# Self-attention of a decoder kernel: rounded three-product projections, values for two heads at a time, output projection with stationary weights

## The reference

```python
# one head of 16, per sequence of 56 tokens
q = n @ Wq[h] + bq[h]          # 448 x 128
k = n @ Wk[h] + bk[h]
v = n @ Wv[h] + bv[h]
s = q @ k.T + slope[h] * alibi # causal
p = softmax(s)
y += (p @ v) @ Wo[h]           # 448 x 256
# after all heads
x = x + y + bo
```

## Time and profile before

| | us |
|---|---|
| median of 3 runs | 560.01 |
| lowest and highest | 556.16, 560.06 |
| the profiled execution, its device time | 554.69 |
| its span, first to last instruction | 553.1 |
| TensorE busy in the span | 521.2 (94%) |
| VectorE busy | 338.2 (61%) |
| ScalarE busy | 297.1 (54%) |
| mean granted clock of TensorE | 0.985 |

### The profile page before, as it was taken

The page is one execution under the profiler, slowest core; times in us unless marked ns, Lnnn a source line. Parts: engine busy times, 40 slices in busy tenths (PEclk is TensorE's granted clock), DMA queues, the critical chain, the costliest instruction groups (busy, mean ns, idle before and its releaser), DMA issues.

```text
span 553.1 us, 16214 instructions
## 1 busy us (share of the span) xinstructions
PE 521.2 (94%) x7083; PEld 411.2 (74%) x7083; DVE 338.2 (61%) x757; ACT 297.1 (54%) x521; POOL 4.1 (1%) x12
## 2 busy tenths in 40 slices
PE   7999999999978999999999998999999899888897
PEld 6777777787857888878788877779778688645356
DVE  3335645665425676557665678855678764778961
ACT  3363655434325675557766667766557755353132
POOL 1000000000010000000000000000000000000000
PEclk9999999999979999999999999999999999899989
DMA  8821212212500211121111111111111100000000
GB/s 278 364 77 40 77 38 77 58 58 77 201 9 2 65 51 39 42 76 39 39 39 41 39 39 39 39 41 38 40 39 39 48 2 2 2 1 10 0 1 17
DMA packets 10791, 30.83 MB, mean 56 GB/s; under 512 B 1377, under 2 KB 4450, under 8 KB 9954
## 3 DMA queue, kind: packets, MB, share of 16 engines
q1 hardware_dynamic: 10274, 29.07, 16.1%
q0 software_dynamic: 192, 0.51, 0.3%
q10 hardware_dynamic: 256, 0.23, 0.1%
HBM read 29.35 MB, written 0.46 MB: 54 GB/s over the span
## 4 chain that ended last, share of the span: by engine, by line
PE 73%; DVE 11%; ACT 9%; issue 3%; DMA 2%; SPq 0%; DVEq 0%; ACTq 0%
PE psb L1213 10%; PE psb L1223 10%; PE psa L1145 8%; PE psa L1265 7%; PE psb L1283 5%; PE pst L1160 5%; PE psa L1153 5%; PE psb L1189 3%; PE psa L1169 2%; PE psb L1492 2%; ACT shared L520 2%; PE pst L1431 2%; DMA cst<-consts_dram 1%; PE psb L1180 1%; PE pst L1349 1%
## 5 line engine op out<-in xcount | busy, mean ns | idle before, releaser
L1213 PE MATMUL psb<-cx,wkv 128*128 128x500 f32 x288 | 78.1, 407 | 4.1 <-ACT vmem L371 4.1
L1223 PE MATMUL psb<-wkv,cx 128*125 128x256 f32 x552 | 77.5, 289 | 3.6 <-ACT kx L364 3.6
L1223 PEld LDWEIGHTS psb<-wkv,cx 128*125 128x125 f32 x552 | 68.4, 186 | 7.6 <-ACT kx L364 6.1
L1213 PEld LDWEIGHTS psb<-cx,wkv 128*128 128x128 f32 x288 | 50.6, 188 | 16.9 <-ACT vmem L371 4.6
L371 ACT ACTIVATE vmem<-psb 125x512 f32<-125x512 f32 x46 | 27.5, 597 | 57.9 <-PE psb L1223 57.9
L1265 PE MATMUL psa<-qb,kx 32*125 32x112 f32 x1536 | 54.7, 279 | 1.4 <-ACT vmem L371 0.8
L812 DVE TENSOR_SCALAR shared<-shared,top 125x896 f32<-125x896 f32 x48 | 30.8, 684 | 40.0 <-ACT shared L520 39.8
L313 ACT ACTIVATE shared<-shared,negmax 112x112 f32<-112x112 f32 x64 | 24.0, 376 | 55.0 <-DVE negmax L728 55.0
L1265 PEld LDWEIGHTS psa<-qb,kx 32*125 32x125 f32 x1536 | 46.3, 183 | 9.6 <-issue 4.8
L1145 PE MATMUL psa<-xnT,whd 128*128 128x448 f32 x128 | 50.9, 540 | 0.8 <-DVE xnT L662 0.8
L812 DVE TENSOR_SCALAR smem<-smem,top 125x896 f32<-125x896 f32 x48 | 30.8, 683 | 27.7 <-ACT smem L520 27.4
(11 more groups left out here) (299 smaller groups left out, 799.2 us busy)
## 6 DMA issues: line engine op xcount, KB each, us to landing
ring<-ctx_t_dram SPq DMA_DIRECT2D x24, 500.0 KB, 3.7
whd<-heads_dram SPq DMA_DIRECT2D x16, 385.0 KB, 3.2
whd<-heads_dram SPq DMA_DIRECT2D x16, 129.0 KB, 2.3
wraw<-w_dram SPq DMA_DIRECT2D x2, 1024.0 KB, 6.2
mats_sb<-mats_dram SPq DMA_DIRECT2D x1, 1536.0 KB, 14.6
wraw<-gate_dram SPq DMA_DIRECT2D x1, 1024.0 KB, 8.1
wraw<-up_dram SPq DMA_DIRECT2D x1, 1024.0 KB, 10.2
wraw<-down_dram SPq DMA_DIRECT2D x1, 1024.0 KB, 12.1
```

What stands on the lines that cost most here:

```text
L1213: last = nc.tensor.matmul(bank[:, 0:UT], wkv[a][:, 0, c, m * P:(m + 1) * P], cx[b][u % 2][:, c, :], start=(a == b and c == 0), stop=(a == ...
L1223: last = nc.tensor.matmul(bank[0:CT, t * D:(t + 1) * D], cx[b][u % 2][:, c, a0:a0 + CT], wkv[a][:, 1, c, :], start=(a == b and c == 0), st ...
```

## The change

- q and k are computed by three f32r products (`PARTS0`: HI x HI, LO x HI, HI x LO), 12 matmuls of 448 columns a head. The normalised x is divided once, into `x0[HI]` and `x0[LO]`. The weights of each head are divided during the loop: `split_qk(h + 2)` on ScalarE behind `pT` of head h, `rest_qk(h + 2)` on VectorE behind the normalisation of head h. The parts share memory with the context tiles `cx`.
- Values are computed for two heads at a time, 256 columns a matmul, in three products: `project_v(n, i)` is one tile of 112 tokens, 6 matmuls; head h issues `project_v(h + 2, 0)` before its transposes and `project_v(h + 2, 1)` behind them. The weights of a pair are divided by `split_v` and `rest_v` in odd heads.
- The output projection has the weights stationary: 2 matmuls of 448 columns, giving the transposed output `yT`. After the last head it is evicted with its bias by ScalarE and VectorE and turned back by `turn_y(t)`, once before the cross-attention and three times within its loop. The bias matmuls at the start are gone.
- Transfers: q and k weights, value weights of a pair, output weights and biases are separate; the load of `down` stands behind the loads of heads 2 and 3, each with a wait for the rests that free the buffers.
- Moved: `wkv[HI]` and `round_up(0)` from heads 7 and 8 to head 14, `round_up(1)` to head 15 between the exponentials and `pT`; `wkv[LO]` to head 14, `remainder(0)` to head 15, `remainder(1)` between `normalise1(0)` and `finish1(0)`.

```diff
+            load_qk(1)
+            load_v(1)
+            load_wo(0)
+            load_wo(1)
...
+            for i in range(2):
+                sp.wait_ge(s_wl, i + 1)
+                load_qk(2 + i)
+                sp.wait_ge(s_vl, i + 1)
+                load_v(2 + i)
             sp.dma_start(wraw[:, 2, :], down).then_inc(s_wff, 16)
...
+            def split_qk(h):
+                act.wait_ge(s_w[h % 2], 16 * (h // 2) + 16)
+                if h >= 2:
+                    act.wait_ge(s_q, 2 * h - 2)
+                nc.scalar.activation(cq[HI][h % 2], whd[h % 2][:, 0:QW], ACT.Copy).then_inc(s_wh, 1)
+
+            def split_v(j):
+                act.wait_ge(s_wv[j % 2], 16 * (j // 2) + 16)
+                if j >= 2:
+                    act.wait_ge(s_v, 2 * j - 2)
+                nc.scalar.activation(wkv[HI][:, j % 2, :, :], vraw[j % 2], ACT.Copy).then_inc(s_vh, 1)
...
             root(0, n=NT)
+            split_qk(0)
             act.wait_ge(s_nb, 1)
...
             for h in range(H0):
                 head(h)
+                if h + 2 < H0:
+                    split_qk(h + 2)
+                if h % 2 and (h + 3) // 2 < H0 // 2:
+                    split_v((h + 3) // 2)
...
+            def rest_qk(h):
+                dve.wait_ge(s_wh, h + 1)
+                nc.vector.tensor_tensor(cq[LO][h % 2], whd[h % 2][:, 0:QW], cq[HI][h % 2].bitcast(F32), ALU.subtract).then_inc(s_wl, 1)
...
                 nc.vector.tensor_tensor(pn, pm, rinv[:, :].unsqueeze(2).to_broadcast([TT, NT, TT]), ALU.mult).then_inc(s_pn, 1)
+                if h + 2 < H0:
+                    rest_qk(h + 2)
+                if h % 2 and (h + 3) // 2 < H0 // 2:
+                    rest_v((h + 3) // 2)
                 prepare(h)
-                if h + 1 < H0:
-                    move_v(h + 1)
+                if h + 2 < H0:
+                    move_v(h + 2)
...
             def project_qk(h):
-                pe.wait_ge(s_w[h % 2], 16 * (h // 2) + 16)
+                pe.wait_ge(s_wl, h + 1)
                 for part in range(2):
                     if h:
                         pe.wait_ge(s_qe, 2 * h - 1 + part)
+                    for a, b in PARTS0:
+                        for c in range(DC):
+                            if h == 0 and part == 0:
+                                pe.wait_ge(s_xnTd if b else s_xnT, c + 1)
+                            last = nc.tensor.matmul(PS[0][:, part, 0:TOK], cq[a][h % 2][:, (c * 2 + part) * P:(c * 2 + part + 1) * P], x0[b][:, c, :],
+                                                    start=(a == b and c == 0), stop=(b == LO and c == DC - 1))
+                    last.then_inc(s_q, 1)
...
             def output(h):
+                pe.wait_ge(s_wo[h % 2], 16 * (h // 2) + 16)
                 pe.wait_ge(s_oe, h + 1)
-                for t in range(NT):
-                    last = nc.tensor.matmul(yrow(t), oT[:, t * TT:(t + 1) * TT], whd[h % 2][:, OB:OB + D], start=False,
-                                            stop=False, skip_group_check=True)
+                for m in range(DC):
+                    last = nc.tensor.matmul(pst[:, m, 0:TOK], whd[h % 2][:, QW + m * P:QW + (m + 1) * P], oT[:, :], start=(h == 0), stop=(h == H0 - 1))
                 last.then_inc(s_y, 1)
...
+                if h + 2 < H0:
+                    project_v(h + 2, 0)
                 pe.wait_ge(s_pn, 2 * h + 2)
...
-                if h + 1 < H0:
-                    project_v(h + 1)
+                if h + 2 < H0:
+                    project_v(h + 2, 1)
                 pe.wait_ge(s_te, h + 1)
```

More of the change, by code:

```diff
@@ L36, with decoder @@
 NEG = -1.0e30
[L37 to L40, removed]
+QW = DC * 2 * P
+HW = 4 * D + 4
 HI, LO = 0, 1
 PARTS = ((HI, HI), (HI, LO), (LO, HI))
-def decoder(nc, x, ctx_t, mask, heads, mats, qkv1, proj1, gate, up, down, w1, w2, rows, single, cols,
+PARTS0 = ((HI, HI), (LO, HI), (HI, LO))
+def decoder(nc, x, ctx_t, mask, wqk, wvp, wo, hbias, mats, qkv1, proj1, gate, up, down, w1, w2, rows, single, cols,
             scal, consts, out):
@@ L233, in _ @@
                 sp.dma_start(ctxs[u], ctx_t[u]).then_inc(s_ctx[u], 16)
[L235 to L239, removed]
+            for h in range(H0 - 1):
+                if h:
+                    sp.wait_ge(s_y, h)
+                    load_wo(h + 1)
+                if h + 4 < H0:
+                    sp.wait_ge(s_wl, h + 3)
+                    load_qk(h + 4)
+                if h % 2 and (h + 7) // 2 < H0 // 2:
+                    sp.wait_ge(s_vl, (h + 5) // 2)
+                    load_v((h + 7) // 2)
             sp.wait_ge(s_ter, 3)
@@ L741, in head @@
                     dve.wait_ge(s_y, h)
-                nc.vector.tensor_scalar_add(oT[:, :], PS[2][:, 1, 0:TOK], whd[slot][:, VB:VB + 1]).then_inc(s_oe, 1)
+                nc.vector.tensor_scalar_add(oT[:, :], PS[2][:, 1, 0:TOK], hb[:, h, 2:3]).then_inc(s_oe, 1)
             move_v(0)
+            rest_qk(1)
+            move_v(1)
+            rest_v(1)
             for h in range(H0):
@@ new lines, in project_qk, with project_v @@
+                    last.then_inc(s_q, 1)
+            def project_v(n, i):
+                j, t = n // 2, 2 * (n % 2) + i
+                if i == 0:
+                    pe.wait_ge(s_vl, j + 1)
+                    if n >= 2:
+                        pe.wait_ge(s_ve, n)
+                bank = kvb if n == 1 else A2
+                for a, b in PARTS:
+                    for c in range(DC):
+                        last = nc.tensor.matmul(bank[0:TT, i * D:(i + 1) * D], x0[b][:, c, t * TT:(t + 1) * TT], wkv[a][:, j % 2, c, :],
+                                                start=(a == b and c == 0), stop=(a == LO and c == DC - 1))
+                if i:
+                    last.then_inc(s_v, 1)
@@ L1242, in project_q, with turn_y @@
                 last.then_inc(s_qx, 1)
+            def turn_y(t):
+                pe.wait_ge(s_ye, 1 + (t > 0))
+                pe.wait_ge(s_yed, 1 + (t > 0))
+                dst = T1 if t else A0
+                for c in range(DC):
+                    last = nc.tensor.transpose(dst[0:TT, c * P:(c + 1) * P], yT[:, c, t * TT:(t + 1) * TT], ident)
+                last.then_inc(s_yt, 1)
+            turn_y(0)
             pe.wait_ge(s_wkv, 1)
@@ L1395, in project_out @@
                 pe.wait_ge(s_xbe, 2 * t + 2)
[L1396 removed]
+                nc.tensor.matmul(T1[0:TT, 0:D], ones[0:1, 0:TT], single_sb[0:1, 1, :], start=True, stop=False)
                 for c in range(DC):
@@ L1569, in _ @@
             turn_context(3)
-            nc.tensor.matmul(A3[0:TT, 0:D], ones[0:1, 0:TT], single_sb[0:1, 1, :], start=True, stop=False)
+            nc.tensor.matmul(A3[0:TT, 0:D], ones[0:1, 0:TT], single_sb[0:1, 0, :], start=True, stop=False)
             turn_divided(3)
@@ L1626, in _ @@
             pe.wait_ge(s_xbe, 8)
-            nc.tensor.matmul(A1[0:TT, 0:D], ones[0:1, 0:TT], single_sb[0:1, 2, :], start=True, stop=False)
+            nc.tensor.matmul(A1[0:TT, 0:D], ones[0:1, 0:TT], single_sb[0:1, 1, :], start=True, stop=False)
             for c in range(DC):
```

162 lines of the change are left out of this document (92 added, 70 removed).

## The result

| | before | after |
|---|---|---|
| median of 4 runs, us | 558.09 | 581.65 |
| lowest and highest | 552.52, 560.06 | 581.43, 582.46 |
| profiled execution, span | 553.1 | 579.6 |
| first transposes of head 0 to those of head 15 | 132.3 | 153.5 |
| mean granted clock | 0.985 | 0.962 |

The changed kernel is slower by a factor of 1.046, 95% interval 1.042 to 1.050. The two medians alone give 1.042; the four runs of the kernel before lie up to 7.5 us apart. The forecast was 583, range 567 to 597. The span grew by 26.5 us: 3.5 before head 0 (its transposes start at 25.56, had 22.05), 21.1 in the loop, 0.7 from head 15 to the first scores of the cross-attention (16.04 us, 15.37 from the earlier trace rows), 1.2 behind them.

The account below looks back on a forecast made before the run. TensorE bound the loop only because VectorE's side work ran ahead of the transposes. Start 3, loop 15.3, end 0.9 and 0.7, clock 5 sum to 24.9 us: 579.6 from 554.7, 585 from the median 560.0; forecast 583, range 567 to 597.

Parts of the forecast that it names:

- What binds: Self-attention loop: TensorE binds, at 8.78 us a head, only because VectorE's side work sits ahead of the transposes.
- Passes: Each head: split at T + 1.02, rest T + 1.72, 0.60 per rest; 12 f32r passes 2.60 us; quiet heads 8.57 and 9.17.
- Prepare: VectorE between rest_qk and oT: preparation, hidden before, is all exposed, 0.88 to 3.69 us in heads 3 to 6, 8 to 10.
- Clock: Loop: TensorE's waits make the clock fall, taken as two falls at 2.5 us, 5 us; bounds 0 and 17.
- Loop: Transposes of head 0 to those of head 15: intervals sum to 147.7 us against 132.3, a loss of 15.3 without clock falls.
- Start: Before head 0: split_qk(0) waits for first weights, landing at 9.3, and the clock is likely to fall: 3 us lost.
- End: Way to the cross-attention scores: yT evictions, turn_y(0) and remainder(1) between normalise1(0) and finish1(0) add 0.9 us.
- Behind the scores of the cross-attention: Cross-attention loop bound by TensorE: three more turn_y with hand-overs add 0.7 us.
- Transfers: Loads: same bytes, issued a head or more before use, cost nothing; a late down would hold the exponentials of head 1.
- The rival on the other side: Loop: VectorE's rests not in the way, oT starts by T + 2.3, TensorE stays the bound: 550 us, chance 0.10.

Follow-up runs that it names:

- the run with the other start: The changed kernel with split_qk(0) on ScalarE behind xn of tiles 2 and 3 instead of ahead of them: 579.61 us, ratio 1.042.
- the last version: Changed kernel with rests under the exponentials, split_qk(0) behind xn, weight sums behind head 3, dummy matmuls before transposes of heads 14 and 15: 546.91 us, ratio 0.983.

## Why the prediction was right, and which terms were off

- **What binds.** Right: the loop was bound by TensorE only because the side work of VectorE ran before the transposes. Putting a wait ahead of that side work turned the bound over; with the rests added to the kernel before, the loop is 154.7 us without any change of TensorE's work.
- **Passes.** The split starts at T + 1.03 (1.02 forecast), the rest at T + 1.68 (1.72), each rest adds 0.60 to the spacing, and `rest_v` sets odd heads 0.6 above even ones: 9.03 and 8.44 in heads 11 and 12. The f32r pass of 448 columns was put at 2.60 us for 12. It is less: in head 7, where the clock stays up, the passes start 0.207 us apart, 2.48 for 12, which is just under the stated lower bound of 2.52. It is 4.76 us from `output` (104.85) to the next transposes (109.61), against the 4.91 of the sum. That 0.15 is why the quiet heads came out 0.1 below. The 0.26 us that the prediction read for a pass of 500 columns is the recorded length of a group shared over its six; from start to start the trace before has 0.228 (median). By the gap of the Trainium skill (TensorE: Matmul & The Clock Gate, Back-to-back issue gap) this stretch would be an estimated 4.53, further off than the sum from the rows.
- **Prepare.** Right: heads 3, 6 and 9, whose intervals hold no clock fall, are 9.96, 9.34 and 11.42 against 10.07, 9.45 and 11.67. Moving it took 20.1 us out of the loop, an estimated 6.5 of them the clock's.
- **Clock, the mis-sized term.** The estimate was two falls at 2.5 us, with bounds 0 and 17. There were five, at 1.60 to 1.69 us: 8.2 us instead of 5. (Four prices come from the run with dummies; the fifth, of head 5, from the run with the other start, where this head takes 11.04 us without a fall: 1.63.) The number was too low: falls stand at the waits of 3.0 to 4.3 us in heads 4, 5, 8 and 10 and at the stall of the scores in head 2, where TensorE's longest idle time is 1.3 us. Head 9, with 3.6 us, has none, and with the other start it is heads 5 and 10 that have none. So the length of a wait does not decide by itself whether the clock falls, and what does is not shown. The price was too high, because each fall lasted 3.4 us and not the 6.9 of the earlier trace rows, so half of it, 1.7, is the most that it can cost.
- **Loop.** Without the falls 153.5 - 8.2 = 145.3 against the summed 147.7. Of these 2.4 us, 0.5 are head 2 (9.98 without its fall, 10.45 forecast) and the rest 0.1 to 0.25 in nearly all of the others. The two errors, 2.4 down and 3.2 up, nearly cancel: 21.1 us lost in the loop against 20.3 forecast. The closeness of the total is partly this luck.
- **Start.** 3.5 us against 3. The mechanism held (split waits for weights that landed at 9.6, forecast 9.3, and the clock fell). But T of head 0 lies between 25.6 and 28.3 in the profiled executions of the forms that keep this start, so the term is known to 3 us at best.
- **End.** 0.7 against 0.9. `remainder(1)` (L742) stands between the moments of tile 0 and its normalisation, as forecast. But in the profiled executions of the forms with this same end the stretch takes 15.6 to 16.7 us, with the clock down for 3.4 or 6.8 us of it, so the agreement is within what one execution can tell.
- **Behind the scores of the cross-attention.** 1.2 against 0.7, and the cause is another. The 0.7 was for three more `turn_y`. In the five changed forms whose clock is down for 6.8 us behind the cross-attention, this stretch takes 383.0 to 383.2 us, against 383.4 in the kernel before, which also has 6.8. In the four where it is down for 10.2 or 10.3 us, the changed kernel among them, it takes 384.5 to 384.7. So `turn_y` costs nothing that shows, and the 1.2 us are a longer fall. The two falls, before and after:

```profile
479.30:486.10 6.80, 6.80 (x16) 2.87 (x15) 5.53 (x21) 1.36 (x5) 0.00 (x0) 0.50 0.00 0
502.30:512.60 10.30, 9.81 (x27) 5.94 (x29) 6.89 (x20) 2.56 (x9) 0.00 (x0) 0.50 0.01 2
```

- **Transfers.** Right for this kernel: the table of waits between 25 and 171 us has no wait of ScalarE for a transfer. The sign that the prediction gave, `down` late, showed only later, and mainly in the last version.

The rival on the other side (TensorE stays the bound, 550 us) failed on its condition, since `oT` came late. With `oT` in time, the same work runs at 550.8 us, but that this is nearly its 550 is luck. It counted 10 us down from 560.0, and the measured form lies 5.2 below the 555.97 of its own chip. Its loop gained 11.1 us, where 14.3 were put. In its profiled execution the start then lost 5.7 us.

## What to carry to other kernels

An engine with half its time idle can still be the bound through one position in its queue: before adding a pass, write down what it waits for, and what that wait is put in front of. Put side work whose inputs are ready ahead of an instruction that waits for another engine, and put an added pass where the engine already waits (here under the exponentials, 1.7 us for 1.2 us of passes). A wait of TensorE can also cost clock, here 1.6 to 1.7 us for each fall of 3.4 us. So price a wait with the slower stretch that may follow it, and expect that two executions of the same loop put these stretches in different places.

## What the runs showed of the hardware

- A clock fall in the loop lasted 3.4 us in the changed kernel, five times of five, and 3.4 or 6.8 to 6.9 us in others; in the earlier trace rows it lasted 6.9, and at the start and behind the cross-attention up to 10.3. In one loop executed with two starts, falls came at different heads though the waits for `oT` were equal to 0.01 us. The page of the Trainium skill "TensorE: Matmul & The Clock Gate" (What's actually happening) has two levels and activity that releases the throttle; the traces agree, with 1.00 and 0.50 to 0.51 as the only levels in stretches that hold no change.
- Dummy matmuls of 64 columns, with one in about 0.23 us, held the clock in heads 2, 4, 8 and 10 (1.00 from 110 to 118 us in head 8), and did not in head 5 (a fall from 82.3 to 85.7).
- The same 188 KB of constants, issued at 1.65 us each time, landed 6.7 to 9.7 us later in the eleven profiled executions, and the first transposes started between 8.4 and 11.4 us. A change at the start has to be read against that spread.
- In all nine profiled executions of the changed kernel and its variants the clock fell once between 9.8 and 11.6 us, for 3.4 to 10.3 us; in the two with the start of the kernel before (itself, and with rests added) it did not. No run shows why.
